# A gated cross-attention and feed-forward layer: one hand-written list of places for all engines, or a table of places for each engine

## The reference

```
xn = layernorm(x);  q = xn@Wq.T+bq;  k = ctx@Wk.T+bk;  v = ctx@Wv.T+bv
s = q.k/4, -inf where mask_SxS2[query,key] or mask_pad[batch,key]
x = x + tanh(g_xattn) * (softmax(s) @ v @ Wo.T + bo)
h = layernorm(x)
y = ((silu(h@gate_w*gate_s) * (h@up_w*up_s)) @ down_w) * down_s
x = x + tanh(g_ffn) * y
```

## Time and profile before

| what | value |
|---|---|
| median of 3 runs | 702.71 us (700.14 to 703.07) |
| the profiled execution | 702.68 us |
| its span, first to last instruction | 700.6 us |
| TensorE busy | 614.2 us, 88% |
| VectorE busy | 511.1 us, 73% |
| ScalarE busy | 369.1 us, 53% |
| GpSimd busy | 237.0 us, 34% |
| mean granted TensorE clock | 0.915 |

### The profile page before, as it was taken

One profiled execution on the slowest core, in us unless ns is written; L12 is line 12 of the kernel. 1 busy time (PEld: TensorE's weight loads), 2 busy tenths in 40 slices (PEclk: granted clock), 3 DMA queues, 4 the chain that ended last, 5 costly groups with the idle time before them and its releaser, 6 DMA issues. The chain is left out here.

```text
span 700.6 us, 14562 instructions
## 1 busy us (share of the span) xinstructions
PE 614.2 (88%) x5133; PEld 351.0 (50%) x5133; DVE 511.1 (73%) x1543; ACT 369.1 (53%) x672; POOL 237.0 (34%) x321
## 2 busy tenths in 40 slices
PE   4737668778798999899998999899999998999997
PEld 3624323323365546554665456554655365456583
DVE  3536787796889877997789777987798798554421
ACT  3434473434464745584466546574566376566261
POOL 2101010101133432443244334253245344437274
PEclk9866775867799999999999999999999999999999
DMA  7495970540153012901090026201350200110000
GB/s 245 184 201 175 225 153 16 128 57 2 46 129 49 10 47 69 138 10 46 33 171 14 11 67 141 46 2 49 90 56 2 61 22 15 41 36 19 16 16 31
DMA packets 52849, 50.25 MB, mean 72 GB/s; under 512 B 6477, under 2 KB 40362, under 8 KB 52778
## 3 DMA queue, kind: packets, MB, share of 16 engines
q1 hardware_dynamic: 52778, 49.32, 30.4%
HBM read 35.15 MB, written 9.44 MB: 64 GB/s over the span
## 5 line engine op out<-in xcount | busy, mean ns | idle before, releaser
L780 DVE CUSTOM_DVE_ANT_0 junk<-sc,mq 128x256 bf16<-128x256 f32 x512 | 185.2, 420 | 43.7 <-PE sc L862 40.8
L789 DVE SCALAR_TENSOR_TENSOR ws<-sc,padc,mask_k 128x1024 f32<-128x1024 f32 x128 | 163.5, 1280 | 55.5 <-issue 46.6
L607 ACT ACTIVATE ws<-ws 128x1024 f32<-128x1024 f32 x128 | 135.2, 1057 | 44.0 <-DVE ws L789 41.5
L477 POOL TENSOR_TENSOR ff<-ga,up 128x256 f32<-128x256 f32 x96 | 69.9, 728 | 159.9 <-DVE ga L750 159.8
L987 PE MATMUL work<-h_h,wg 128*128 128x256 f16 x384 | 90.5, 276 | 7.4 <-DVE cl L700 7.2
L597 ACT ACTIVATE up<-work,fuse_s 128x256 f32<-128x256 f32 x96 | 45.4, 473 | 97.5 <-PE work L987 96.6
L987 PE MATMUL work<-h_h,wu 128*128 128x256 f16 x384 | 92.1, 279 | 0.0
L987 PE MATMUL work<-h_l,wu 128*128 128x256 f16 x384 | 92.1, 279 | 0.0
L987 PE MATMUL work<-h_l,wg 128*128 128x256 f16 x384 | 90.3, 275 | 0.0
L887 PE MATMUL av<-ws,va 128*32 128x256 f32 x1024 | 90.2, 427 | 0.0
L999 PE MATMUL work<-wd,f_h 128*128 128x512 fp8e4 x192 | 73.0, 380 | 0.0
(11 more groups left out here) (122 smaller groups left out, 1030.8 us busy)
## 6 DMA issues: line engine op xcount, KB each, us to landing
qs<-q_scratch SPq DMA_DIRECT2D x48, 128.0 KB, 6.8
cin<-in_ctx SPq DMA_DIRECT2D x8, 512.0 KB, 4.8
xin<-in_x SPq DMA_DIRECT2D x8, 512.0 KB, 6.2
xb<-in_x SPq DMA_DIRECT2D x8, 512.0 KB, 3.7
att_u<-un SPq DMA_DIRECT2D x128, 32.0 KB, 2.4
out_x<-yt SPq DMA_DIRECT2D x16, 256.0 KB, 2.0
ks<-k_scratch SPq DMA_DIRECT2D x48, 64.0 KB, 5.0
q_scratch<-qh SPq DMA_DIRECT2D x8, 256.0 KB, 2.3
```

The lines of the kernel that those rows point to most:

```text
L477: pool.tensor_tensor(ff[:, n % RING, :], ga[:, n % RING, :], up[:, n % RING, :], ALU.mult).then_inc(ff_done, 1)
L607: act.activation(ws[:, unit, :, :], ws[:, unit, :, :], ACT.Exp, scale=1.0 / SSC).then_inc(exp_done, 1)
L780: last = dve.tensor_tensor_reduce(junk[:, HPG * t + j, :], sc[k][:, place(j)], mq[p_][:, t, :], 1.0, -3.4e38, ALU.add, ALU.max, mx[:, t, c ...
L789: dve.scalar_tensor_tensor(out=ws[:, 2 * (u % 2) + kt, :, :], in0=sc[kt][:, :].rearrange("p (j l) -> p j l", j=HPG), scalar=padc[par][:, k ...
```

## The change

The single list goes. Each engine gets a table of its own (`PE_AT`, `ACT_AT`, `DVE_AT`, `POOL_AT`, `SP_AT`) with a place for each of its pieces, tables for the pieces of batch 0 (`PE_0` and so on), and places for the setup conversions and for the twelve slabs of feed-forward weights. `order` sorts them; only the order within an engine matters.

The order that comes out on TensorE in a steady batch begins (scores of batch 2): `maxima12.3 scores3.3`, and around the output projection reads `xT0.4 down_b1.0 mrow1.2 xT1.4 maxima0.3 scores7.2 out0.1 maxima1.3 out1.1 cT0.4 cT1.4 weighted2.2 scores8.2 maxima2.3 q0.4 weighted3.2 scores9.2 maxima3.3 x2T0.1 x2T1.1 q1.4 scores10.2 maxima4.3 k0.4 gu0.1`, where the number behind the point is the batch. The first `gu` of a batch stands at place 51.9 where it stood at step 59. Before it, TensorE has done 11 units of `scores` of the next batch and 5 of `maxima` of the one after (before: 14 and 8), and `cT`, both `q` and `k` of the batch behind them (before: of these only `q` 0).

At the end TensorE's order is `weighted7.7 gu9.6 gu10.6 gu11.6 down_a0.6 down_a1.6 spread0.7 down_b0.6 spread1.7 down_b1.6 out0.7 out1.7 x2T0.7 x2T1.7 gu0.7 ...`. Before it was `... out0.7 gu11.6 out1.7 down_a0.6 down_a1.6 x2T0.7 down_b0.6 x2T1.7 down_b1.6 gu0.7 ...`.

Further: the maxima always use `sc[0]` and the scores always `sc[1]`, each unit after the one before it has been read; the three work banks are given out in rotation, the one used longest ago first; both halves of a `weighted` group are done together; `q` is written and fetched in two halves with semaphores of their own; `out` starts on the first half of `at`; Wo is loaded at the start into `ws`; eight small loads, with the identity, Wk and Wv among them, are issued by ScalarE; the slabs are loaded later.

```diff
-WHEN = { ("load_c", 0): -64, ... }
+PE_AT = {
...
+    "scores": [-3.252, -1.573, -0.77, -0.094, 2.619, 5.453, 10.866, 14.631, 16.546, 17.254, 19.024, 20.578, 21.633,
+               22.444, 22.638, 24.429],
...
+    "out": [46.907, 47.478],
+    "x2T": [49.85, 50.106],
+    "gu": [51.872, 52.555, 53.418, 54.295, 54.637, 55.78, 55.984, 59.685, 61.161, 62.728, 63.39, 65.024],
+    "down_a": [67.14, 67.197],
+    "down_b": [69.711, 77.051],
 }
...
+def order(table, first, more=()):
+
+    places = [(first.get(name, row)[n] if b == 0 and n < len(first.get(name, row)) else at + STEPS * b, name, n, b)
+              for name, row in table.items() for n, at in enumerate(row) for b in range(NB)]
+    places += [(at, name, n, 0) for name, row in more for n, at in row.items()]
+    return [place[1:] for place in sorted(places)]
...
+def bank_uses():
+    counts, last, held, uses = [0] * 3, [-1] * 3, {}, {}
+    for at, (name, n, b) in enumerate(PE_ORDER):
+        if name in IN_BANKS or name == "down_a":
+            i = min((i for i in range(3) if i not in held.values()), key=lambda i: last[i])
+            uses["down" if name == "down_a" else name, n, b] = i, counts[i]
...
-            sp.dma_start(ident[:, :], ident_in).then_inc(ld_ident, 16)
-            sp.dma_start(st_k[:, :], Wk).then_inc(ld_wk, 16)
             sp.dma_start(cin[:, :, :], c_v[0]).then_inc(ld_c, 16)
...
+            sp.dma_start(st_o[:, :, :], Wo.rearrange("(t p) i -> p t i", p=P)).then_inc(ld_wo, 16)
...
+                if name == "put_q":
+                    wait_free(sp, "q", n, b)
+                    past(sp, qs_in[n], 96 * b)
...
+            act.dma_start(ident[:, :], ident_in).then_inc(ld_ident, 16)
+            act.dma_start(st_k[:, :], Wk).then_inc(ld_wk, 16)
...
+                    past(pe, m_free, 16 * b + n)
+                    for j in range(HPG):
+                        pair, at = 2 * g + j // 2, 64 * (j % 2)
+                        last = mm(sc[0][:, place(j)], qs[b % 2][at:at + 3 * HD, pair, t * P:(t + 1) * P],
+                                  ks[b % 2][at:at + 3 * HD, g, :], start=True, stop=True)
...
+                    past(pe, t_free, 16 * b + n)
...
+                        last = mm(sc[1][:, place(j)], ks[b % 2][at:at + 3 * HD + 2, g, kt * P:(kt + 1) * P],
+                                  qs[b % 2][at:at + 3 * HD + 2, pair, :], start=True, stop=True)
...
+                if name == "out":
...
+                        if n == 0 and k % 2 == 0:
+                            pe.wait_ge(at_ready, 2 * b + k // 2 + 1)
```

More of the change, by code:

```diff
@@ L44 @@
 STEPS = 32
-SUMS_AT = (1, 2)
-WHEN = {
[3 rows of a table removed]
[L52 to L58, removed]
-}
@@ L73 @@
[L73 to L76, removed]
-}
[L80 to L101, removed]
+FIRST = -64
@@ new lines @@
+DVE_AT = {
+    "maxima": [-16.741, -14.658, -12.39, -10.934, -9.586, -7.272, -5.77, -5.3, -5.189, -3.616, -3.233, 0.42, 2.439,
+               5.12, 7.833, 13.153],
+    "scores": [-3.223, -1.307, 1.214, 3.063, 6.668, 9.761, 14.486, 15.423, 18.397, 20.539, 24.215, 26.176, 26.332,
+               26.734, 26.815, 28.39],
+    "stats1": [-67.961],
+    "shift1": [-67.215],
+    "xT": [-49.465, -48.562],
+    "q": [-43.604, -41.013],
+    "cT": [-44.898, -43.96],
+    "k": [-37.865],
+    "v": [-25.247],
+    "recip": [36.41],
+    "spread": [39.304, 44.505],
+    "out": [47.712, 49.762],
+    "shift2": [50.622],
+    "x2T": [53.075, 53.107],
+    "gu": [58.242, 58.254, 58.711, 58.779, 59.207, 60.233, 60.75, 60.781, 62.377, 67.678, 68.292, 69.055],
+    "down": [77.119, 79.012],
+}
@@ new lines @@
+POOL_AT = {
+    "power": [-5.961, 98.828],
+    "pad_row": [19.45],
+    "padc": [39.259],
+    "mrow": [43.726, 66.71],
+    "add_bo": [97.916],
+    "split_att": [97.131, 97.31],
+    "fuse": [102.723, 103.795, 103.882, 107.694, 109.259, 122.067, 122.092, 122.148, 125.969, 128.628, 128.632,
+             128.799],
+    "fsplit": [103.97, 104.003, 122.07, 122.07, 122.113, 124.254, 125.111, 127.968, 128.044, 128.645, 128.657,
+               128.808],
+    "add_y": [129.352, 154.081],
+}
+SP_AT = {
+    "load_x": [-105.793],
+    "load_c": [-80.717],
+    "put_q": [-51.836, -43.924],
+    "put_k": [-49.028],
+    "get_k": [-39.808],
+    "get_q": [-48.421, -21.282],
+    "rows": [-16.516, 9.539],
+    "gather": [15.416, 21.502],
+    "load_xb": [12.314],
+    "den": [18.649],
+    "store": [84.171, 84.784],
+}
@@ new lines @@
+DVE_ORDER = order(DVE_AT, DVE_0, [("setup", SETUP_DVE), ("gates", {0: GATES_DVE}), ("mask", {0: MASK_DVE})])
+POOL_ORDER = order(POOL_AT, POOL_0)
+SP_ORDER = order(SP_AT, SP_0, [("slab", SLAB_SP)])
+IN_BANKS = ("xT", "q", "cT", "k", "v", "spread", "out", "x2T", "gu")
+def bank_uses():
[4 more added lines that the diff above has]
+            uses["down" if name == "down_a" else name, n, b] = i, counts[i]
+            counts[i], last[i] = counts[i] + 1, at
+            if name == "down_a":
+                held[n, b] = i
+        if name == "down_b":
+            last[held.pop((n, b))] = at
+    return uses
@@ L104, in three, with av_uses @@
+def av_uses():
+    uses = [piece for piece in PE_ORDER if piece[0] in ("weighted", "mrow")]
+    return {piece: n for n, piece in enumerate(uses)}, dict(zip(uses[1:], uses))
+USE, (AV_USE, AV_BEFORE) = bank_uses(), av_uses()
 def three(w_h, w_l, d_h, d_l):
@@ L109, in past @@
 def past(eng, sem, count):
-    if not isinstance(count, int) or count > 0:
+    if count > 0:
         eng.wait_ge(sem, count)
@@ L672, in tile_stats, with variance @@
                 dve.bn_stats(bst[which][:, t, :], src[:, t, :]).then_inc(stats[which], 1)
-            def piece(name, n, b, odd):
-                bank = bank_of(name, n)
+            def variance(which, b):
+                dve.wait_ge(stats[which], 2 * (b + 1))
+                for t in range(TT):
+                    last = dve.bn_aggr(mv[which][:, t, :], bst[which][:, t, :])
+                last.then_inc(bnagg[which], 1)
+                dve.wait_ge(bnagg[which], b + 1)
+                dve.tensor_scalar(ve[which][:, :], mv[which][:, :, 1], 1e-5, 1.0 / (SX * SX), ALU.add,
+                                  ALU.mult).then_inc(vareps[which], 1)
@@ L806, in _ @@
[L806 removed]
+                    dve.tensor_tensor(yt[:, n, :], bank[:, :], dsb[:, :], ALU.mult).then_inc(freed, 1)
         @block.tensor
@@ L1001, in piece @@
                     if half:
[L1002 to L1022 removed]
+                        last.then_inc(ready, 1)
 _INS = ["x", "ctx_2048", "mask_SxS2_bc0", "mask_BxS2_bk0", "g_xattn", "g_ffn", "L0_xattn_Wq", "L0_xattn_bq",
```

1048 lines of the change are left out of this document (501 added, 547 removed), and 3 rows, old and new, of the table WHEN.

## The result

The changed kernel takes 643.05 us (640.01 to 643.64, 4 runs) where the kernel before takes 702.89 beside it: ratio 0.9146, interval 0.9117 to 0.9176. That is 60 us faster.

What follows compares the result with a forecast made beforehand. VectorE with its gaps was taken to bound the fill, TensorE the steady batches. Terms -12 (start), 0 (score banks), -14 (fill), -16 (rotation), +7 (tail) sum to -35: span 665.6, time 668 us, range 648 to 692.

Steps and rivals of the forecast that it cites:

- The fill: First scores to first `gu`: VectorE's 91 us of work at a share of 89%, 102 us; -14, bounds -4 and -21.
- The start: Setup to first maxima: first half of `q` sent by itself, first maxima at 36 us; -12, bounds 5 and 16 earlier.
- the single score banks: First maxima to first scores: waits for turns set against fewer maxima and saved waits; 0, bounds 5 us either way.
- the rest with the tail: End of the kernel: TensorE idle about 7 us between `out` and `x2T`, then slower `gu`; +7, bounds +4 and +10.
- 70 to 71 us a batch is the floor, and no order can go below it: Steady batch on TensorE: summed work 69.4 us, row less waits and lost clock 70.9 us.
- the term of -16 for the steady stage: Behind 193 us: 24 us of losses before, 8 left; -16, bounds -24 and +5.
- rival C: Whole kernel: fill reaches 96%, steady stage its floor, tail costs 4; 650 us or a little less, chance 0.15.
- my sum: Steady batch: TensorE's pieces added up at full clock, 69.4 us, as a check.
- Work banks in rotation: Behind 193 us: a piece waits for the use three places back, not its own bank's last; -16.
- A (turns take over): Steady stage: single score banks make VectorE and TensorE wait for each other, 82 us a batch; 710 to 735, chance 0.08.
- B: Whole kernel: only the start gives, steady stage keeps its losses and fill its 81%; 698 us, chance 0.07.
- the forecast: Whole kernel: 655 to 690 us, chance 0.70.

## Why the prediction was wrong

**The direction was right, two sizes were not.** The fill and the steady batches gave 57 us where 30 were given. The start (-13.2 for -12), the single score banks (+0.6 for 0) and the rest with the tail (+7.5 for +7) met their numbers, in part by luck. Of the start, which I had put down in good part to the first half of `q` going by itself, only 2 us are that. The tail has the mechanism named, idle time between `out` and `x2T` (4.58 us), before `gu` (1.46 us) and a `gu` at half clock behind it. But the rest begins at the last of the five GpSimd pieces, long before the tail, and there the steady gain is missing: the clock is 0.95 from 441 to 510 us and TensorE idles for 3.1 us from 510 to 560, of which the sum had nothing.

**The step that failed** is the sentence "70 to 71 us a batch is the floor, and no order can go below it", on which the term of -16 for the steady stage and rival C's bound rested. A batch takes 67.0 us with the same work. Of the 33.2 us of four batches, 17 are the waits and the clock that I had seen (4 x 4.3), and 16 lie below the floor. It failed twice over. First, I took TensorE's busy time for its work: 75.2 less the waits the trace shows. I split a batch by kind of piece, from the start of one group of matmuls to the start of the next (own arithmetic from the timelines; a group carries what is lost before the next one):

| us a batch | before | old places, rotation | after | my sum |
|---|---|---|---|---|
| maxima and scores | 13.2 | 10.7 | 9.1 | 10.2 |
| `weighted` | 10.1 | 8.3 | 8.0 | 9.1 |
| `gu` | 23.3 | 23.9 | 22.1 | 22.2 |
| `down` and `out` | 16.2 | 16.2 | 15.9 | 15.6 |
| the rest | 12.5 | 13.7 | 11.8 | 12.3 |
| sum | 75.2 | 72.8 | 66.9 | 69.4 |

Of the 8.3 us a batch 4.1 come from maxima and scores and 2.1 from `weighted`, both just the short pieces that stand between others. Of these 6.2 us the trace of the kernel before shows 2.5 as idle time: the 1.81 us of the earlier trace rows stand behind a unit of scores, and 0.65 us before `cT` 1 behind a half of `weighted`. Of the 1.2 us of `gu`, all may be the clock that falls behind the first. The other 3.7 us were counted as busy. I priced nothing there: the halves of `weighted` together, an edit that I had listed, had no term, and alone it gives 1.9 us a batch. Second, the sum that should have been a check used 0.32 us for a unit and 0.57 for a half as if they were the work. Each was taken between two other pieces and has the change in it: in the changed kernel a whole `weighted` group takes 1.0 us, not 1.14, and a unit of scores with maxima right behind it 0.23. The sum came to 69.4 all the same, 1.5 under the row, and I raised it to the row instead of asking what the row had too much.

**"Work banks in rotation" was the wrong name for the term.** Rotation by itself gives 0.3 us a batch on the old places; -16 for it in the whole stage would have needed some 3. Its value is that it permits the new places, without which it is worth little, and they without it cost 148 us more than with it. The same holds for the score banks (81 us). "I count 0" for these was right only because the places were made for them. The waits of the earlier trace rows and their clock, 4.0 to 4.3 us, are half of the 8.3 us of a batch, and they are gone. But they weren't to be had one by one: taking the first away in the kernel before made it slower.

**The fill.** I had 91 us of VectorE's work at a share of 89%. From the first scores to the first `gu` the windows read, before and after:

```profile
76.56:192.96 116.40, 86.50 (x661) 36.87 (x659) 94.06 (x301) 54.97 (x78) 14.19 (x17) 0.69 0.41 83
```

```profile
64.00:156.60 92.60, 72.39 (x642) 37.64 (x643) 85.72 (x276) 55.62 (x78) 10.90 (x14) 0.76 0.47 132
```

The work is 85.7 us and the share 92.6%. So of the 10 us that I missed, some 6 are work and 4 are share. The work before was 94.06 us, not 96.7, for my window began 2.6 us ahead of the first scores. It then fell by 8.3 us, not 5.5: four units of scores fewer (26, not 30), and the `cT` and `k` that I added for batch 3 didn't come on top. The waits of VectorE in the fill, 74 to 193 us before and 62 to 163 after:

```profile
DVE ws L789 <- issue: 12.8, 7, 4.0
DVE junk L780 <- PE sc L862: 8.5, 4, 3.7
```

```profile
DVE ws L736 <- PE sc L893: 3.9, 6, 1.5
DVE junk L724 <- PE sc L883: 2.8, 5, 0.8
```

With two smaller rows after (0.8 us) and one before (0.4) they fell from 21.7 to 7.5 us. But the reason given, an order of VectorE's own, is not it: with its maxima, scores and `gu` in TensorE's order the fill takes 93.8 us. Each of places, score banks and rotation is needed here too: without the one it took 116.9 us, without the others 112.9 and 119.6.

**The rivals.** A (turns take over) did not come in this kernel, but its mechanism was found where banks and places don't fit: 763 us with own banks on the old places, 728 with turns on the new. The first has 81.6 us a batch beside A's 82, though by fewer and longer waits than A had. B fell: the start is a fifth of the gain. C was right in its direction, and its end, 650, was tied to the false floor; with 66.9 a batch for its 71 it would have come out at 630 to 634 us (4 to 5 batches of 4 us less, worked out afterwards), so the measured time lies between C so mended and the forecast.

**What stays open.** Of the 5.9 us a batch between old places with rotation and new ones, 2.9 are idle time by the windows above (5.74 of 140 us against 0.22). The other 3.0 are counted as busy; how much of them is changes between kinds of piece and how much short waits that the records cover could not be split. Only the 0.1 us for a change of `weighted` was measured by itself. The rest of the start's 13 us was seen to go with the old places, but with slabs placed ahead of the context, so their shares weren't told apart.

## What to carry to other kernels

Busy time of a pipelined TensorE is no floor: add up a batch from groups that stand in long rows of their own kind, and where the row is above the sum, the difference may be to be had. Buffers and order are one design: a part of such a change tested alone may cost more than the whole gives (own score banks on the old places cost 77 us, the whole change gave 60), so read each bank's chain of users in the order that will run. Where an idle gap has been filled, look for who is late next before counting its whole length: here `x2T` started no earlier with 4.4 us of gap filled, and came some 4 us earlier when GpSimd's sum was moved too. What the time gained by that can't be told from the scatter of the runs.

## What the runs showed of the hardware

Small loads issued by a second engine at the same time as large ones landed later (VectorE's first piece at 9.19 us) than the same loads issued ahead of them on one queue (6.50 us). A fetch of the queries in two halves of 64 KB took 2.4 us from issue to landing in the median in the changed kernel, where one of 128 KB took 6.8 in the kernel before. The size isn't all of it: the same halves took 4.2 us with the old places and fixed banks. The changed kernel, the kernel before and that one:

```profile
qs<-q_scratch SPq DMA_DIRECT2D x96, 64.0 KB, 2.4
```

```profile
qs<-q_scratch SPq DMA_DIRECT2D x48, 128.0 KB, 6.8
```

```profile
qs<-q_scratch SPq DMA_DIRECT2D x96, 64.0 KB, 4.2
```

And a change between kinds of matmul pieces, measured on `weighted` and `gu` alone, cost about 0.1 us that the profile counts as busy.
